# A twelve-layer perceiver on one core: where the rescaling factors of streamed attention stand in PSUM and in the queue

## What is computed

```python
x = x + _L0_xattn_ref(_layernorm(x), ctx, ...)   # causal
x = x + _L1_xattn_ref(_layernorm(x), ctx, ctx, mask, ...)
x = x + _L3_xattn_ref(_layernorm(x), ctx, ctx, ..., theta, gate)

q = split_heads(x_q @ Wq + bq) * dp_scale
k = split_heads(x_kv @ Wk + bk)
v = split_heads(x_kv @ Wv + bv)
attn = jax.nn.softmax(jnp.einsum('bhic,bhjc->bhij', q, k), axis=-1)
o = jnp.einsum('bhij,bhjc->bhic', attn, v)
return o @ Wo + bo
```

## Time and profile before

| | |
|---|---|
| three executions | 1695.16, 1699.74, 1701.62 us; median 1699.74 |
| the profiled execution | 1697.52 us, span of its profile 1695.7 us |
| granted TensorE clock, mean | 0.975 of full speed |
| TensorE matmuls | 1591.1 us busy, 94% of the span |
| VectorE | 1032.1 us, 61% |
| ScalarE | 948.0 us, 56% |
| GpSimd | 697.0 us, 41% |

### The profile page before, as it was taken

How to read it: one execution, slowest core, us unless ns; L and a number is a source line. 1 busy time by engine, 2 the same in 40 slices (tenths; PEclk the granted TensorE clock), 3 DMA queues, 4 the chain that set the end, 5 groups by cost and what they waited for, 6 DMA issues and landing times. The chain is left out here.

```text
span 1695.7 us, 48967 instructions
## 1 busy us (share of the span) xinstructions
PE 1591.1 (94%) x20179; PEld 1364.2 (80%) x20179; DVE 1032.1 (61%) x1430; ACT 948.0 (56%) x1834; POOL 697.0 (41%) x625
## 2 busy tenths in 40 slices
PE   6999999999887999999999898998699999999987
PEld 5888888888665888898888676976488898888863
DVE  7667787885356877677777343013676666666633
ACT  4677777777413466666665612311267777777752
POOL 5655555551004655554554000000275555555302
PEclk9999999999988999999999989989999999999999
DMA  7675555554135776555554353970375555555440
GB/s 178 165 194 134 121 139 132 130 124 106 58 115 122 186 202 158 138 145 133 146 142 116 79 203 122 320 269 35 101 170 149 136 133 129 127 137 128 105 118 4
DMA packets 149248, 235.46 MB, mean 139 GB/s; under 512 B 24200, under 2 KB 64516, under 8 KB 148100
## 3 DMA queue, kind: packets, MB, share of 16 engines
q1 hardware_dynamic: 141090, 225.09, 50.6%
q10 hardware_dynamic: 7938, 7.23, 1.6%
HBM read 107.06 MB, written 0.23 MB: 63 GB/s over the span
## 5 line engine op out<-in xcount | busy, mean ns | idle before, releaser
L1305 DVE TENSOR_REDUCE L_xattn_maxima<-L_xattn_ps 128x4 f32<-128x1024 f32 x588 | 691.3, 1219 | 321.4 <-PE L_xattn_ps L877 317.6
L1067 ACT ACTIVATE L_xattn_p_ring<-L_xattn_ps 128x512 f32<-128x512 f32 x1176 | 674.3, 598 | 343.3 <-PE L_xattn_ps L926 328.0
L926 PE MATMUL L_xattn_ps<-L_xattn_q_packed,L_xattn_k_packed 128*128 128x256 f32 x2352 | 451.9, 298 | 9.8 <-ACT L_xattn_p_ring L1067 4.7
L926 PEld LDWEIGHTS L_xattn_ps<-L_xattn_q_packed,L_xattn_k_packed 128*128 128x128 f32 x2352 | 335.2, 190 | 71.6 <-issue 35.9
L962 PE MATMUL L_xattn_ps<-L_xattn_p_ring,L_xattn_v_ring 128*17 128x128 f32 x9408 | 289.3, 273 | 1.0 <-ACT L_xattn_p_ring L1067 1.0
L845 PE MATMUL L_xattn_ps<-L_xattn_ctx_halves,L_xattn_w_halves 128*128 128x256 f32 x1764 | 260.9, 286 | 1.5 <-POOL L_xattn_ctx_halves L1224 1.5
L962 PEld LDWEIGHTS L_xattn_ps<-L_xattn_p_ring,L_xattn_v_ring 128*17 128x17 f32 x9408 | 242.4, 97 | 23.5 <-ACT L_xattn_p_ring L1067 1.6
L849 PE MATMUL L_xattn_ps<-L_xattn_w_halves,L_xattn_ctx_halves 128*128 128x256 f32 x1764 | 259.6, 285 | 0.0
L1239 POOL TENSOR_TENSOR L_xattn_k_ring<-L_xattn_k_full,consts 128x512 fp32r<-128x512 f32 x147 | 154.9, 1054 | 223.5 <-ACT L_xattn_k_full L1080 115.3
L1221 POOL TENSOR_TENSOR L_xattn_ctx_halves<-L_xattn_ctx_chunk,consts 128x512 fp32r<-128x512 f32 x129 | 134.2, 1040 | 261.0 <-DMA L_xattn_ctx_chunk<-in_ctx_chunks 177.2
L845 PEld LDWEIGHTS L_xattn_ps<-L_xattn_ctx_halves,L_xattn_w_halves 128*128 128x128 f32 x1764 | 233.3, 193 | 4.6 <-issue 2.6
(11 more groups left out here) (380 smaller groups left out, 1160.3 us busy)
## 6 DMA issues: line engine op xcount, KB each, us to landing
L_xattn_k_packed<-L_xattn_k_ring SPq DMA_DIRECT2D x588, 128.0 KB, 2.4
L_xattn_ctx_chunk<-in_ctx_chunks SPq DMA_DIRECT2D x147, 256.0 KB, 3.3
L_xattn_k_packed<-L_xattn_k_ring SPq DMA_DIRECT2D x588, 64.0 KB, 2.2
L_ffn_W<-in_experts_W SPq DMA_DIRECT2D x16, 1024.0 KB, 13.7
L_xattn_mask_chunk<-L_xattn_mask ACTq DMA_DIRECT2D x49, 128.0 KB, 3.0
weights<-in_pack_L_attn SPq DMA_DIRECT2D x10, 512.0 KB, 4.8
L_xattn_ctxT<-in_ctxT SPq DMA_DIRECT2D x5, 896.0 KB, 8.1
L_xattn_ctx<-in_ctx SPq DMA_DIRECT2D x5, 896.0 KB, 8.3
```

The costliest lines, as they stand in the source:

```text
L926: last = pe.matmul(L.ps[:, bank, d * 2 * S:(d + 1) * 2 * S], self.k_packed[s][:, quarter, d, half * P:(half + 1) * P], q[:, 2 * pair:2 * p ...
L1067: act.activation(self.p[t % P_RING][:, 4 * quarter:4 * quarter + 4, :], L.ps[:, E_BANK[unit], :].rearrange("p (h n) -> p h n", n=S), ACT.Exp)\
L1305: dve.tensor_reduce(out[:, 4 * v:4 * v + 4], L.ps[:, M_BANK + 2 * v:M_BANK + 2 * v + 2, :] .rearrange("p b (k n) -> p (b k) n", k=2), AX_X ...
```

## The change

In turned steps b = 1 to 10 (`borrows`: steps 6 to 48) the transposition and the factors leave banks 0 and 1. The transposition goes into bank 2 and the factors into bank 4, which belong to the batches of maxima, at a time between the two batches of that step. They wait for VectorE instead of ScalarE: the transposition for the first half of the step's first batch, the factors for its second half. The second batch of that step waits for the factors' exponential as well. Units 5, 6 and 7 take banks 1, 0 and 1 in turn. The factors' matmuls move from behind the last projection part to its middle (behind three of its six matmuls), and ScalarE's exponential of the factors moves ahead of its drain of the values. The steps of b = 0, 11 and 12 stay as they are. No arithmetic changes.

```diff
--- before.py
+++ after.py
@@ -574,11 +574,21 @@
     return 6 if step < NCHUNK else 8
 
 
+def borrows(step):
+
+    return LAG <= step < NCHUNK
+
+
 def e_order():
 
     at, bank, before, used = {}, [], [], {}
 
     def unit(key, step):
+        if key[0] != "scores" and borrows(step):
+            before.append(-1)
+            at[key] = len(at)
+            bank.append(M_BANK if key[0] == "turned" else M_BANK + 2)
+            return
         free = E_BANKS if step < NCHUNK else E_BANKS + (KV_BANK,) if step < NCHUNK + 2 else TAIL_BANKS
         b = min(free, key=lambda i: (used.get(i, -1), free.index(i)))
         before.append(used.get(b, -1))
@@ -858,7 +868,10 @@
             return
         L, batch, slot, bank = self.L, 2 * n + d, n % K_RING, self.L.ps[:, M_BANK:M_BANK + 4, :]
         cornered = self.causal and n == NCHUNK - 1
+        b = block_turned(step)
         pe.wait_ge(L["q_heads_ready"], d + 1)
+        if d == 1 and b and borrows(step):
+            pe.wait_ge(L["e_drained"], E_AT["factor", b] + 1)
         if d == 0:
             pe.wait_ge(L["k_hi_ready"], n + 1)
             if self.masked:
@@ -931,17 +944,23 @@
 
     def pe_turned(self, pe, b):
 
-        L, unit = self.L, E_AT["turned", b]
+        L, unit, step = self.L, E_AT["turned", b], turn_step(b)
         pe.wait_ge(L["stage_ready"], b + 1)
-        self.pe_bank_free(pe, unit)
+        if borrows(step):
+            pe.wait_ge(L["batch_reduced"], 4 * (step - 1) + 1)
+        else:
+            self.pe_bank_free(pe, unit)
         pe.transpose(L.ps[0:64, E_BANK[unit], 0:S], self.stage[:, :], self.net.const("identity"))\
           .then_inc(L["e_filled"], 1)
 
     def pe_factor(self, pe, b):
 
-        L, unit = self.L, E_AT["factor", b]
+        L, unit, step = self.L, E_AT["factor", b], turn_step(b)
         pe.wait_ge(L["e_drained"], E_AT["turned", b] + 1)
-        self.pe_bank_free(pe, unit)
+        if borrows(step):
+            pe.wait_ge(L["batch_reduced"], 4 * (step - 1) + 2)
+        else:
+            self.pe_bank_free(pe, unit)
         for i in range(4):
             last = pe.matmul(L.ps[:, E_BANK[unit], i * S:(i + 1) * S],
                              self.net.spread[:, 4 * i:4 * i + 4, :].rearrange("p h n -> p (h n)"),
@@ -1013,9 +1032,10 @@
                 if b is not None:
                     self.pe_turned(pe, b)
                 self.pe_unit(pe, m, 5)
-                self.pe_project(pe, step, 3)
+                self.pe_project(pe, step, 3, 0, 3)
                 if b:
                     self.pe_factor(pe, b)
+                self.pe_project(pe, step, 3, 3, 6)
                 self.pe_unit(pe, m, 6)
                 self.pe_batch(pe, step, 1)
                 self.pe_unit(pe, m, 7)
@@ -1189,12 +1209,14 @@
             for u in range(3, 9):
                 if u == turned_before(step) and b is not None:
                     self.act_turned(act, b)
-                if u == factor_before(step) and b:
+                if u == factor_before(step) and b and not borrows(step):
                     self.act_factor(act, b)
                 if u < 8:
                     self.act_unit(act, m, u)
                 if self.masked and u == 3 and 2 <= step + 2 < NCHUNK:
                     self.load_mask(act, step + 2)
+                if u == 5 and b and borrows(step):
+                    self.act_factor(act, b)
                 if u == 5:
                     self.act_drain_v(act, step)
             self.act_round_context(act, step + 3)
```

## The result

| | kernel before | changed kernel |
|---|---|---|
| seven executions each, us | median 1696.78 (1692.98 to 1701.62) | median 1709.12 (1703.88 to 1710.63) |
| span of the profiled execution | 1695.7 | 1708.5 |
| granted TensorE clock in it, mean | 0.975 | 0.967 |

The ratio is 1.0058, with a 95% interval of 1.0042 to 1.0075: slower by 7 to 13 us, about 10.

What follows compares the result with a forecast made beforehand. TensorE was busy 94%, with VectorE closing the loop behind the second batch. First stage +2.5, masked +2.7 and third 0 summed to +5.2 us: 1702.7 for the profiled execution, 1705 on the median's scale, range 1696 to 1712.

Steps and rivals of the forecast that it cites:

- Step 1: Transposition in bank 2 waits for the first batch's first half: released at 209.12 against 209.08, nothing that counts.
- Step 2: Unit 5 takes unit 3's bank, drained long before: its wait and restart go, 0.36 us by itself.
- Step 3: Factors' matmuls in bank 4 wait for the first batch's second half: start at 210.27, where the queue alone gives 209.80.
- Step 4: ScalarE's factors' exponential moves ahead of its values' drain; factors' matmuls last 0.66 us with a restart, exponential ends at 211.56.
- the restart: Restart of the factors' matmuls after waiting: taken as 0.10 us; none would make the sum +2.8, twice that +7.6.
- Step 5: Second batch waits for the factors' exponential: starts at 211.61 instead of 211.30, loss 0.31 us, no slack in VectorE's loop.
- early blocks: Turned steps whose VectorE reductions end early, so nothing waits: second batch 0.27 us earlier, 0.34 with the third stage's slack.
- Step 6: Unit 7's wait goes, worth nothing because VectorE's loop covers it; the values' drain keeps some 0.3 us of cover.
- The count: 24 of 30 blocks late: nine in the first stage, ten masked, five in the third.
- rival C: More blocks early as L1326 starts ahead of L1239: +1.8 or -3.4 us, 1696 to 1702; chance 0.13.
- rival B: All blocks late, second batch behind the factors' exponential: +9.1 us, 1709, or 1712 with the larger restart; chance 0.18.
- A: Unit 5's waits go in all 30 steps and nothing takes their place: -10.8 us, 1689; chance 0.12.

Runs made afterwards that it cites:

- run 3: Changed kernel with only the transposition in a borrowed bank, factors in banks 0 and 1, no added wait: 1687.01 us against 1700.09 for the kernel before.
- run 2: Changed kernel's new order alone, everything in banks 0 and 1 with the old waits: 1698.89 us against 1700.09 for the kernel before.
- Run 4: Changed kernel with the factors in bank 3, waiting for the first half, added wait kept: 1698.1 us against 1700.09 for the kernel before.
- run 8: Kernel before with only the second batch's added wait for the factors' exponential: 1716.88 us against 1699.07 for the kernel before.
- run 6: Changed kernel with GpSimd's keys' rounding waiting for VectorE's shift update in turned steps: 1698.36 us against 1699.07 for the kernel before.
- run 1: Changed kernel with its banks and waits, but factors and their exponential in the old order: 1710.03 us against 1700.09 for the kernel before.
- run 5: Changed kernel again, unedited, in a second set (the second trace): 1703.48 us against 1699.07 for the kernel before.

## Why the prediction was right

**Step 1** (the transposition waits for the first half: nothing that counts). Right: it stands 5.99 us behind the start of its step (202.93 to 208.92), where it stood 5.95 (203.13 to 209.08), and 0.04 is what the prediction had.

**Step 2** (0.36 us go at unit 5). Right. The trace shows unit 5 at 0.03 behind the transposition, nearer than the 0.12 named; it takes 0.31 of the queue (208.95 to 209.26) instead of 0.24, so the two together take 0.34 for a forecast 0.36. Run 3, which keeps this and the order and drops the rest, brings the batch 0.36 nearer in the block shown, and gained 8.9 us over run 2 and 10.2 over the kernel before, against 10.8.

**Step 3** (the factors wait for the second reduction). Right: 0.14 to 0.15 us behind its end, for a forecast 0.17; a hole of 0.43 us, within 0.4 to 0.5. Run 4 replaced this wait alone by one for the first half, and the batch came 0.47 sooner.

**Step 4.** Right: the factors last 0.64 (forecast 0.66 with a restart); of the queue they take 210.05 to 210.53, 0.48, against 0.40 without a stop. The unknown of the sum, the restart, is 0.08 here, not far from unit 5's 0.10. ScalarE follows by 0.03.

**Step 5** (the added wait delays the second batch by 0.31). Right in its mechanism, and run 8 shows that a delay there passes through. The batch stands 2.50 behind the transposition, against a forecast of about 2.5 (211.61 less 209.08 is 2.53). One term of it was too small: from ScalarE's end to the batch 0.10 us, where I took unit 5's 0.05; the terms of steps 3 and 4 were a little too large and made up for it. The early blocks lie at 2.03 rather than near 1.95, mostly for the same reason (0.05 of it, and 0.04 for factors that last 0.60 instead of 0.56). They still gain: a turned step of 8.66 us against 8.99.

**Step 6** (unit 7's wait is worthless). Right: unit 7 now follows the batch by 0.44 instead of 0.56, and the step's own length grew by 0.20 only (9.27 against 9.07); but the next step's first batch stands 2.32 behind its keys' start (212.20 to 214.52) instead of 2.24, and takes back 0.08 of the 0.12. The loop reads 0.60 + 2.36 + 0.14 = 3.10 us (211.42 to 212.02, the reductions, and to 214.52), against 3.14. The drain of the values ends at 211.81, with 0.39 us of cover.

**The count.** 24 late were assumed, 23 and 21 came. The prices: 0.27 us for nine of the ten masked blocks (9.34 to 9.61 us a turned step), the forecast's 0.27, and with the early block of the first stage at -0.33, (2.6 + 0.33) / 9 = 0.33 for a late one there (0.31). A block that flips in the third stage was worth 0.33 + 0.34 = 0.67 in the forecast and is 9.27 less 8.66 = 0.61 in the traces; one and three flips make -0.6 and -1.8, and the third stage shows -0.7 and -1.9 for a forecast of 0. That is rival C's mechanism, in small.

The five and five of the third stage were luck. The traces have 2, 4, 5, 8 and 9 long ones there in kernels with the steps of before or of the change, and with the forecast's prices nine would have made the sum about +7.9 and two +3.2. The first +5.0 is as near to +5.2 as it is because the one flip (-0.6) and the 0.65 us of the masked step 10 cancel; the second trace, without that step and with three flips, has +3.0.

**What was off.** The sum said +5.2, the steps say +5.0 and +3.0, but the medians +9.9 and +6.3 by the ratio. No term of the sum failed beyond what is said above; missing was one for what the rest of the program does, and the +9.9 is almost twice the forecast. In the first profile 7.5 us of the 7.8 beyond the steps lie in two untouched stretches at a lower granted clock (0.98 to 0.86, 0.95 to 0.92). In the second profile the tail is 3.7 us longer too (105.3), but other untouched parts are shorter, and the span is +3.4 for +3.0 in the steps. At equal clock the second set has +3.1, the steps' own value. For the first set the clocks of the kernel before are not on record; against a line through the 67 executions of the later sets the changed kernel's seven are +7.9, so some 3 us stay unexplained there. What decides in an execution how much of it runs at the lower level was not found. That 1709 lies in the range is therefore luck in part: the upper end was put at 1712 for rival B, not for this.

**The rivals.** A (waits go, nothing in their place) fell: the factors start 0.15 behind the end of VectorE's second reduction, as the rows had it, and not before. It became true in run 3, which removed what stood against it. B (all blocks late, 1709) has the measured median and is still not what happened: seven blocks were early, and the steps are +5.0, not +9.1. A median alone would have passed for its proof. C (more blocks early) happened for one to three blocks; run 6 made it happen for all 20 outside the masked stage, and its steps gave -2.85 for the -3.4 that stood there.

## What to carry to other kernels

A buffer that is borrowed from another producer brings that producer's release with it, and the lender's next use brings a second wait: compare the release times of both owners before moving, and move only the piece whose new owner is already done (here the transposition's move was worth 9 us, 10 with the new order, and that of the factors cost 13 to 15). Where a loop over a second engine closes without slack, price an edit by where it puts the one instruction that starts the loop. Judge such a price by distances between marks inside the touched steps, or by times at equal granted clock, since the rest of a long program can move by as much as the effect. Where an instruction lies within some nanoseconds of flipping between two lengths, take its count from more than one trace.

## What the runs showed of the hardware that I had not expected

- The release differs by which engine gives and takes: 0.14 to 0.15 us from VectorE's reduction to TensorE (209.91 to 210.05), 0.10 from ScalarE's exponential to a batch (211.32 to 211.42, and 0.09 and 0.10 in runs 1 and 8), though unit 5 followed an exponential by 0.05 before, 0.03 from TensorE's end to ScalarE.
- VectorE's last operation of the update (128x16) takes 0.18 us or up to 1.06, by a few nanoseconds. In the ten traces without run 6's wait it is long (0.89 to 1.06) wherever GpSimd's rounding began 0.006 us or more ahead of it, and short wherever that lead was 0.005 or less; where both start within 0.005 of each other the rounding takes 1.08 or 1.09 instead of 1.04. The Trainium skill ("SBUF — State Buffer", "SBUF: two separate sides") says that whichever of the two starts first holds the shared ports for its whole instruction; run 6, which set the order, agrees. The same section limits this to VectorE operations with two SBUF inputs, against a GpSimd operation that reads SBUF, or in a two-port performance mode, and the reductions agree: they read PSUM, and take 2.36 us beside the rounding in run 6 (205.22, rounding from 205.36) as without it.
- Untouched parts of one program differ between profiled executions: steps 0 to 8 of the masked stage 61.15 to 66.38 us (runs 5 and 8), the tail 101.6 to 106.3, while steps 9 to 48 of the kernel before repeat within 0.1 us in 978.
